# Two-layer gated block on one core: first attention layer and first expert layer rearranged (fills, one-hots, table sums, normalisations, down product)

## The reference, cut to what matters

```python
x = x + tanh(g_xattn[0]) * attn0(layernorm(x), ctx)      # causal, 16 heads of 16, 8 batches of 512 tokens
x = x + tanh(g_ffn[0])   * moe0(layernorm(x))            # 32 experts, top 8, capacity 256, hidden 192, SiLU gate
x = x + tanh(g_xattn[1]) * attn1(layernorm(x), ctx)      # not causal, rows masked
x = x + tanh(g_ffn[1])   * moe1(layernorm(x))            # 8 experts, top 2, capacity 1024, hidden 1024
# moe0: for a token t and each of its 8 experts e: pos = how many earlier tokens chose e
#       buf[e, pos] = x[t]  (dropped at pos >= 256)
#       h = silu(buf @ gate.T) * (buf @ up.T);  out[t] += weight[t, e] * (h @ down.T)[e, pos]
```

## Time and profile before

| | |
|---|---|
| time, median of 3 runs | 2199.86 us (2195.2 to 2203.82) |
| the profiled execution's own time | 2197.13 us |
| its span, first to last instruction | 2195.6 us |
| TensorE busy | 1856.5 us (85%) |
| VectorE busy | 1168.9 us (53%) |
| ScalarE busy | 809.3 us (37%) |
| GpSimd busy | 725.5 us (33%) |
| mean granted clock of TensorE | 0.938 |

### The profile page before, as it was taken

One profiled execution on the slowest core, in us unless ns is written; L12 is line 12 of the kernel. 1 busy time (PEld: TensorE's weight loads), 2 busy tenths in 40 slices (PEclk: granted clock), 3 DMA queues, 4 the chain that ended last, 5 costly groups with the idle time before them and its releaser, 6 DMA issues. The chain is left out here.

```text
span 2195.6 us, 30123 instructions
## 1 busy us (share of the span) xinstructions
PE 1856.5 (85%) x10491; PEld 1039.3 (47%) x10491; DVE 1168.9 (53%) x2966; ACT 809.3 (37%) x1652; POOL 725.5 (33%) x540
## 2 busy tenths in 40 slices
PE   2699999989873888854799999999981999999995
PEld 1345555545442666542234444443331566666664
DVE  3577888887755333333787788878721111212111
ACT  1256555555431222211166666666660111111110
POOL 1212333543344666532112222322113233333322
PEclk9899999999985999977799999999995999999998
DMA  3543334322112888742432244324113323233323
GB/s 92 158 121 103 101 117 141 104 71 89 32 41 90 220 208 221 188 76 89 146 97 85 86 132 128 101 61 132 35 45 93 87 73 77 73 77 77 69 27 96
DMA packets 204245, 222.86 MB, mean 102 GB/s; under 512 B 33438, under 2 KB 195231, under 8 KB 203431
## 3 DMA queue, kind: packets, MB, share of 16 engines
q1 hardware_dynamic: 176458, 177.48, 26.3%
q0 software_dynamic: 27648, 43.60, 10.3%
HBM read 155.06 MB, written 86.93 MB: 110 GB/s over the span
## 5 line engine op out<-in xcount | busy, mean ns | idle before, releaser
L804 DVE TENSOR_REDUCE nmx<-mxb 128x1 f32<-128x512 f32 (+3 forms) x1024 | 585.7, 584 | 212.9 <-PE mxb L657 109.8
L712 ACT ACTIVATE pt<-stb 128x512 f32<-128x512 f32 (+3 forms) x1024 | 499.4, 519 | 365.0 <-PE stb L673 200.4
L657 PE MATMUL mxb<-kst,qst 96*128 96x512 bf16 (+4 forms) x1024 | 355.4, 351 | 62.8 <-DVE nmx L804 52.2
L670 PE MATMUL stb<-qst,kst 99*128 99x512 bf16 (+4 forms) x1024 | 346.4, 345 | 2.1 <-ACT pt L712 1.8
L684 PE MATMUL ob<-pt,va 128*32 128x512 f32 (+3 forms) x2048 | 233.0, 527 | 1.6 <-ACT pt L712 1.1
L1390 PE MATMUL e_h_bank<-e_xT,e_w 128*128 128x512 f32 x512 | 224.8, 598 | 6.1 <-ACT e_xT L1430 5.4
L1404 PE MATMUL e_y_bank<-e_w,e_h 128*128 128x256 f32 x1024 | 226.9, 379 | 0.0
L1071 POOL TENSOR_TENSOR qk<-qk,parts 128x1024 f32<-128x1024 f32 x32 | 68.5, 2139 | 445.9 <-ACT qk L745 224.6
L670 PEld LDWEIGHTS stb<-qst,kst 102*128 102x128 bf16 (+1 forms) x1024 | 99.7, 98 | 235.3 <-ACT pt L712 157.9
L1404 PEld LDWEIGHTS e_y_bank<-e_w,e_h 128*128 128x128 f32 x1024 | 192.9, 190 | 31.8 <-issue 7.2
L1544 POOL DMA_INDIRECT x_after_l<-e_y,e_token x64 | 99.6, 1556 | 282.0 <-DVE e_y L1509 267.3
(11 more groups left out here) (218 smaller groups left out, 2608.0 us busy)
## 6 DMA issues: line engine op xcount, KB each, us to landing
qk_parts<-parts SPq DMA_DIRECT2D x16, 1536.0 KB, 6.0
qst<-qk_parts SPq DMA_DIRECT2D x384, 64.0 KB, 2.3
kst<-qk_parts SPq DMA_DIRECT2D x384, 64.0 KB, 2.3
e_w<-in_L_ffn_w SPq DMA_DIRECT2D x16, 1024.0 KB, 7.4
rows<-rows SPq DMA_DIRECT2D x15, 1060.0 KB, 7.5
crow<-in_ctx SPq DMA_DIRECT2D x16, 512.0 KB, 3.8
x_after_l<-xres SPq DMA_DIRECT2D x16, 512.0 KB, 3.2
e_gu_nat<-in_L_ffn_gate_up_proj SPq DMA_DIRECT2D x64, 128.0 KB, 3.1
```

What stands on the lines that cost most here:

```text
L657: last = pe.matmul(out[:, 0:nk], qst[par][0:rows_used, h, qt * P:(qt + 1) * P], kst[par][0:rows_used, h, 0:nk], start=True, stop=not causal)
L670: last = pe.matmul(out[:, q0:S], kst[par][0:ROWS, h, kt * P:(kt + 1) * P], qst[par][0:ROWS, h, q0:S], start=True, stop=not causal)
L712: act.activation(pt[:, u % 8, q_from(kt):S], stb[(STEPS * b + u) % N_ST][:, q_from(kt):S], ACT.Exp, scale=SCALE).then_inc(s["st_free"], 1)
L804: dve.tensor_reduce(nmx[:, qt, h:h + 1], mxb[(STEPS * n + u) % N_MX][:, 0:k_to(qt)], AX.X, ALU.max, negate=True).then_inc(s["max_free"], 1)
```

## The change

1. Fills: the 15 copies of blank rows leave `experts0`; the list `c.spares` now has 19 entries, and SP issues `c.spares[cur::8]` at the end of iterations 0 to 7 of attention 0.
2. One-hots: GpSimd only subtracts (`differ`: lo in 1024 elements, hi in 512 elements a lane), VectorE compares both with 0 (`one_hot`, two instructions). Tiles 1 and 3 of batch 7 are made on VectorE alone. GpSimd's order becomes `place(done, 1)`, `place(done, 2)`, `low(nn, 1)`, `place(done, 3)`, `norm2(prev)`, in both layers.
3. Table: the four tiles of a batch get their own quarter of one bank, their trips move to steps 18, 20, 22 and 24, and VectorE sums once a batch (`enlist`, step 25) over 256 elements; the tile's number is added and the tiles are summed at the end. `("o", 0, 0)` and `normalise(cur, 0)` move from step 25 to 26.
4. Normalisations: x * rstd + (-mean * rstd), on ScalarE, at steps 16, 17, 18, 20 and 31 to 34, in both layers. VectorE makes -mean, GpSimd the product.
5. Experts of layer 0: `down_(e - 1)` and `result(e - 1)` stand where `down_(e)` and `result(e)` stood.

```diff
-    c.spares = (x1[T:T + CAP0, :], table[T:T + CAP0, 0:D], table[T:T + CAP0, D:W0], x3[T:T + SPARE, :])
+    c.spares = (x1[T:T + CAP0, :], table[T:T + CAP0, 0:D], table[T:T + CAP0, D:W0], x3[T:T + SPARE, :],
+                *(rows1[at_:at_ + SPARE, :] for at_ in range(SPARE, 2 * SLOTS, SPARE)))
...
-    0: ("c", 2, 0, 0, 0), 1: ("c", 2, 1, 0, 1), 7: ("list", -2, 0, 0, 0), 24: ("list", -2, 1, 0, 1),
-    30: ("list", -2, 2, 0, 0), 49: ("list", -2, 3, 0, 0), 3: ("k", 2, 0, 0, 0), ...
+    0: ("c", 2, 0, 0, 0), 1: ("c", 2, 1, 0, 1),
+    18: ("list", -2, 0, 0, 0), 20: ("list", -2, 0, 1, 0), 22: ("list", -2, 0, 2, 0), 24: ("list", -2, 0, 3, 0), ...
...
# SP, end of an iteration
-                if layer == 0 and 0 <= it < len(c.spares):
-                    dst = c.spares[it]
-                    sp.dma_start(dst, c.blank[0:dst.shape[0], 0:dst.shape[1]]).then_inc(c.empty0, 16)
+                if layer == 0 and cur is not None:
+                    for dst in c.spares[cur::B]:
+                        sp.dma_start(dst, c.blank[0:dst.shape[0], 0:dst.shape[1]]).then_inc(c.empty0, 16)
...
# TensorE
-                    pe.wait_ge(s["lo_dve" if dve_made else "lo_pool"], made(b, t))
-                    pe.wait_ge(s["hv_rdy"], 4 * b + t + 1)
+                    pe.wait_ge(s["lo_rdy"], 4 * b + part + 1)
...
# ScalarE
+                    if u in (16, 17, 18, 20) and n3 is not None:
+                        norm1_apply(n3, (16, 17, 18, 20).index(u))
+                    if u in (31, 32, 33, 34) and prev is not None:
+                        norm2_apply(prev, u - 31)
+                last = act.activation(xn[:, i, :], xin[:, i, :], ACT.Identity, bias=shift1[:, i:i + 1], scale=rstd[:, i:i + 1])
...
# VectorE
+            def one_hot(b, t):
                 wait(dve, full["list"], 4 * b + t - 1)
+                if on_dve(b, t):          # batch 7, tiles 1 and 3
+                    dve.tensor_tensor(lo1[...], lanes, lo_f, ALU.is_equal)
+                    dve.tensor_tensor(hv[...], lanes, hi_f, ALU.is_equal)
+                    dve.tensor_scalar(hv[...], hv[...], c.tok1[:, 0:1], None, ALU.mult).then_inc(s["lo_rdy"], 1)
+                else:
+                    dve.wait_ge(s["apart_rdy"], apart(b, t))
+                    dve.tensor_scalar(lo1[t % 2][:, :, :], lo_d[t % 2][:, :, :], 0.0, None, ALU.is_equal)
+                    dve.tensor_scalar(hv[t % 2][:, :, :], hi_d[t % 2][:, :, :], 0.0, c.tok1[:, 0:1],
+                                      ALU.is_equal, ALU.mult).then_inc(s["lo_rdy"], 1)
...
-                        if u in (4, 14, 29, 43):
-                            high(done, (4, 14, 29, 43).index(u))
-                        if u in (8, 24, 30, 49):
-                            enlist(done, (8, 24, 30, 49).index(u))
+                        if u in (4, 14, 19, 23):
+                            one_hot(done, (4, 14, 19, 23).index(u))
+                        if u == 25:
+                            enlist(done)
...
# GpSimd
+            def differ(b, t):
                 pool.wait_ge(s["idx_rdy"], b + 1)
+                wait(pool, s["lo_rdy"], 4 * b + t - 1)
+                pool.tensor_tensor(lo_d[t % 2][:, :, :], lanes_128, lo_f_t, ALU.subtract)
+                pool.tensor_tensor(hi_d[t % 2][:, :, :], lanes_64, hi_f_t, ALU.subtract).then_inc(s["apart_rdy"], 1)
...
                 if done is not None:
                     place(done, 1)
+                    place(done, 2)
                 if nn is not None:
                     low(nn, 1)
                 if done is not None:
-                    place(done, 2)
+                    place(done, 3)
                 if prev is not None:
                     norm2(prev)
-                if done is not None:
-                    place(done, 3)
...
# experts0, TensorE (VectorE's result likewise)
-                down_(e)
+                if e > 0:
+                    down_(e - 1)
+            down_(E0 - 1)
...
-                if e % 2:
-                    for at_ in itertools.islice(fills, 1):
-                        sp.dma_start(rows_next[at_:at_ + SPARE, :], rows_next[0:SPARE, :]).then_inc(s["emptied"], 16)
```

More of the change, by code:

```diff
@@ L291, in attention @@
             lo_f, hi_f = t_("lo_f", [P, NT, 8]), t_("hi_f", [P, NT, 8])
+            lo_d = [t_(f"lo_d{i}", [P, 8, P], BF16) for i in range(2)]
+            hi_d = [t_(f"hi_d{i}", [P, 8, N_HI], BF16) for i in range(2)]
             lo1 = [t_(f"lo1_{i}", [P, 8, P], BF16) for i in range(2)]
-            apart = t_("apart", [P, 8, P], BF16)
             hv = [t_(f"hv{i}", [P, 8, N_HI], BF16) for i in range(2)]
-            listed, part_ = t_("listed", [P, N_HI]), t_("part_", [P, N_HI])
+            listed, part_ = t_("listed", [P, NT, N_HI]), t_("part_", [P, NT, N_HI])
+            found, missing = t_("found", [P, N_HI]), t_("missing", [P, N_HI])
         if layer:
@@ L455, in bank_of, with on_dve, apart @@
             return work[BANK[kind, t]]
-        def made(b, t):
-            if b < B - 1:
-                return 4 * b + t + 1
-            return t // 2 + 1 + (0 if t % 2 else 4 * (B - 1))
+        def on_dve(b, t):
+            return b == B - 1 and t % 2 == 1
+        def apart(b, t):
+            return 4 * b + t + 1 if b < B - 1 else 4 * b + t // 2 + 1
         def rows_of(b):
@@ L635, in trip @@
                 elif kind == "list":
-                    dve_made = b == B - 1 and t % 2
-                    pe.wait_ge(s["lo_dve" if dve_made else "lo_pool"], made(b, t))
-                    pe.wait_ge(s["hv_rdy"], 4 * b + t + 1)
+                    pe.wait_ge(s["lo_rdy"], 4 * b + part + 1)
                     for k in range(8):
-                        done = pe.matmul(out[:, 0:N_HI], lo1[t % 2][:, k, :], hv[t % 2][:, k, :], start=k == 0, stop=k == 7)
+                        done = pe.matmul(out[:, N_HI * part:N_HI * (part + 1)], lo1[part % 2][:, k, :], hv[part % 2][:, k, :],
+                                         start=k == 0, stop=k == 7)
                 else:
@@ L752, in evacuate, with norm1_apply, norm2_apply @@
                     done.then_inc(evac[kind], 1)
+            def norm1_apply(n, i):
+                if i == 0:
+                    act.wait_ge(s["rstd_rdy"], n + 1)
+                    wait(act, full["x"], 2 * n)
+                last = act.activation(xn[:, i, :], xin[:, i, :], ACT.Identity, bias=shift1[:, i:i + 1], scale=rstd[:, i:i + 1])
+                if i == NT - 1:
+                    last.then_inc(s["xn_rdy"], 1)
+            def norm2_apply(b, i):
+                if i == 0:
+                    act.wait_ge(s["rstd2_rdy"], b + 1)
+                    if layer:
+                        wait(act, s[f"scat{b % 2}"], 16 * NSCAT * (b // 2))
+                    else:
+                        wait(act, s["row_out"], 16 * b)
+                last = act.activation(rowb[b % N_ROW][:, i, 0:D], xres[:, i, :], ACT.Identity, bias=shift2[:, i:i + 1],
+                                      scale=rstdb[:, i:i + 1])
+                if i == NT - 1:
+                    last.then_inc(s["row_rdy"], 1)
             def route(b):
@@ L954, in route @@
                 else:
[L955 removed]
+                    wait(dve, s["apart_rdy"], 4 * b)
                     dve.tensor_copy(lo_f[:, :, :], lo_u[:, :, :])
@@ new lines, in enlist @@
+            def enlist(b):
+                got = bank_of("list", 0)[:, 0:NT * N_HI].rearrange("p (t h) -> p t h", t=NT)
+                dve.wait_ge(full["list"], 4 * b + 4)
+                wait(dve, s["lchain"], b)
+                if b:
+                    dve.tensor_scalar(part_[:, :, :], got, 0.0, float(S * b), ALU.is_gt, ALU.mult)
+                dve.tensor_tensor(listed[:, :, :], got, listed[:, :, :], ALU.add).then_inc(evac["list"], 1)
+                dve.wait_ge(evac["list"], b + 1)
+                if b:
+                    dve.tensor_tensor(listed[:, :, :], listed[:, :, :], part_[:, :, :], ALU.add).then_inc(s["lchain"], 1)
+                else:
+                    dve.sem_inc(s["lchain"], 1)
@@ L1016, in _ @@
                         norm2_stats(prev, (23, 24, 26, 27).index(u))
-                    if u == 25 and cur is not None:
+                    if u == 26 and cur is not None:
                         normalise(cur, 0)
@@ L1102, in place @@
                     scatter(b, NSCAT // 4 * quarter, NSCAT // 4 * (quarter + 1))
-                elif b < B - 1 or quarter % 2 == 0:
-                    low_bits(b, quarter)
+                elif not on_dve(b, quarter):
+                    differ(b, quarter)
             for it in ITERATIONS:
@@ L1130, in _, with experts0 @@
                     pool.wait_ge(s[f"scat{par}"], 16 * NSCAT * (B // 2))
-def experts0(c, table, gate_up, down, x, rows_next, token):
+def experts0(c, table, gate_up, down, x, token):
     nc = c.nc
@@ L1166, in _ @@
         def _(sp):
-            fills = iter(range(SPARE, 2 * SLOTS, SPARE))
             for e in range(E0):
@@ L1572, in program @@
```

(2 more changed lines are left out.)

133 lines of the change are left out of this document (56 added, 77 removed), and 2 rows, old and new, of the table TRIPS.

## The result

The changed kernel takes 2211.04 us (median of 6 runs, 2205.22 to 2216.42) against 2198.44 us for the kernel before beside it (2192.42 to 2203.82): a ratio of 1.0059, interval 1.0036 to 1.0083. I had forecast 2190 us. It is slower by 0.6%, a little over the half per cent that I set as the bound (the interval reaches down to 0.4%). So the sign was wrong and the range of 2160 to 2218 held. The profiled execution has a span of 2203.5 us, 7.9 more than before.

The account below looks back on a forecast made before the run. TensorE was taken as the bound, with VectorE's hold-ups showing beyond about 2.2 us in layer 0's attention. Terms -33.5 (experts), +26 (iterations 2 to 7), -2 (tail), 0 (rest) gave -9.5 us: 2190 us, range 2160 to 2218.

Parts of the forecast that it names:

- The forecast mechanism of the one-hots: Layer 0, iterations 2 to 5: VectorE waits for GpSimd's differences, 6.3 us at step 14; TensorE idles 6, then 3 us.
- forecast -33.5: Layer 0 experts: later down product and no fills shorten the stage by 37.3 us, 3.8 lost again at the end.
- forecast +30.2 for iterations 2 to 5: Layer 0 attention: one-hot waits and half clock add 8.4 us to each of iterations 2 to 4, and 5 to iteration 5.
- forecast -7, as -4, -1, -2 and 0: Gains of 4 us in iteration 6, 1 in iteration 7, 2 in layer 0's tail, and nothing in the rest.
- The half clock: Layer 0 attention: TensorE runs at 1.2 GHz after the stalls, counted as 3 us an iteration.
- the experts' chain binds: Rival, chance 0.16: GpSimd's adds land later, the experts' cycle is 7.5 us, 19 us come back, 2209 us.
- the wait for `h` at 26.7 us: Layer 0 experts: TensorE's 0.86 us wait before each down product goes, 26.7 us over 31 cycles.
- the fills' traffic at 10.6: Layer 0 experts: late gathers and the half clock after them, put down to the fills, go: 10.6 us.
- the pair of terms "-4" and "-1": Layer 0 attention: iteration 6 gains 4 us, with GpSimd free at its start; iteration 7 gains 1 us.
- "Rest", put at 0: Layer 1 gains 1 us; ScalarE's wait and an extra product and negation at both layers' starts cost 0.5 each: 0.
- GpSimd isn't late: Rival, chance 0.22: iterations 2 to 5 cost what they did before, since VectorE loses under 2.2 us; 2159 us.
- Half clock decides: Rival, chance 0.20: TensorE stays at 1.2 GHz longer, 4.9 us per stall, +27 us, 2217 us.

Follow-up runs that it names:

- run 3: Kernel before plus only the experts' part: later down product and blank-row copies moved into the first attention layer; 0.9865 of the kernel before.
- run 1: Changed kernel with GpSimd, in layer 0, making the differences of tiles 1 and 2 before norm1 and tile 3's before low(nn, 1); 0.9899 of the kernel before.
- run 9: Kernel before and changed kernel, both unedited, profiled again on one chip; 0.9995 and 1.0042 of the kernel before.
- run 10: Kernel before with the later down product alone, blank-row copies still in the experts' stage; 1.005 of the kernel before.
- run 11: Kernel before with the blank-row copies moved into the first attention layer alone, down product unmoved; 0.9974 of the kernel before.
- runs 4 and 6: Changed kernel with GpSimd's differences earlier in layer 0, plus all normalisations on VectorE (0.9945), or only norm2_apply of iterations 7 and 8 there (0.9875).
- run 2: Changed kernel with both normalisations back on VectorE in both layers, GpSimd's order as changed; 1.0081 of the kernel before.

## Why the prediction was wrong

The forecast mechanism of the one-hots held, and the sum did not. The timed runs alone split it so: -30 us for the experts' part with the fills (run 3; forecast -33.5), +35 for the waits that run 1 removed (forecast +30.2 for iterations 2 to 5), and +7 for all the rest, which is run 1 less run 3 (forecast -7, as -4, -1, -2 and 0). Some 3 us of that +7 are still in iterations 2 to 5. So the step that failed is the rest: the last iterations, and a layer 1 put at nothing. The range held partly by luck, since it was set by the stalls and the clock, and the error came from elsewhere.

In the profiles I had -9.5 us on the span and they have +7.9; on one chip, run 9, the same two kernels have +24.0, in executions 10 us under and 2 over their medians. These are the terms, the first pair before the pair on one chip. (My own sum was 0.8 off: 3 x 8.4 + 5 - 4 - 1 is 25.2, and I wrote 26.)

*One-hots in iterations 2 to 5.* Forecast +30.2 (three times 8.4, and 5); measured 8.1 + 8.3 + 8.9 + 6.2 = 31.5, and 35.7 on one chip. Run 1 shows that it was the two waits and what hangs on them: without them 28 us of it are gone. The hold of each comparison by GpSimd is as I read it from the earlier trace rows. The Trainium skill, "SBUF — State Buffer", section "Who interferes with whom", says the same: VectorE and GpSimd share a port pair that one instruction locks for its whole length. The trace agrees with 2.03 and 1.12 us beside GpSimd, and 0.41 and 0.35 alone in run 1. The half clock cost about the 3 us that I had counted, since a mean clock of 0.96 over 79 us is 6.3 us at 1.2 GHz, but in iteration 3 it followed the first stall only.

*The experts.* Forecast -33.5; measured -43.8 in F and +9.1 until the last add, together -34.7. That this is so near the forecast is luck: on one chip it is -33.8 and +10.3, together -23.5, and timed it is -30. Both terms were mis-sized. The cycle is 6.63 us, not 6.90. The end costs 9.1 and not 3.8 because GpSimd is behind when TensorE finishes: the last add but one starts at 958.28, 5.8 us after its result was there (951.52 + 0.99), and I had it start at once. The rival "the experts' chain binds" is thus true at the end alone; a cycle of 7.5 us isn't there. The split of the gain was wrong in kind. I had the wait for `h` at 26.7 us and the fills' traffic at 10.6, as if each could be had alone. Alone, the later product makes the kernel slower (run 10) and the moved fills give 6 us (run 11); together they give 30 (run 3).

*Iterations 6 and 7: the first step that failed.* It is the pair of terms "-4" and "-1". I wrote them on the ground that GpSimd is free at the start of iteration 6. It is free, and so it makes the differences of tiles 0 and 1 back to back just where VectorE has its chain of short casts: 1.81 us for one of 0.18, and TensorE waits 3.55 us for `m` in iteration 7, 2.5 more than before. In iteration 6 the same chain has a cast of 1.59 us, and TensorE waits 2.32 us behind `maxima`. No run moved these differences, so the price of this hold is read from rows and not tested. In iteration 7 `norm2_apply` on ScalarE comes on top, 4.6 to 5.1 us (57.2 against 52.6 and 52.1 in runs 4 and 6), which is tested. Measured +0.6 and +7.0, together 12.6 worse than forecast; on one chip 15.5 worse.

*"Rest", put at 0: the second.* I had taken layer 1 for a place where TensorE is busy anyway and costed ScalarE's normalisations as work between exponentials. That holds where TensorE has `maxima` to do too (0.3 us an iteration measured). In the last iterations it hasn't, and a step with both takes ScalarE 0.97 us. The first pair of profiles gives +17.5 us for layer 1's periods, the pair on one chip +10.1, and runs 1 and 3, on the chip without pauses, +3.0 (443.1 against 440.1). Of this, run 2 bears out about 3 us (52.4 for period 6 against 55.8 in run 1). GpSimd's order in layer 1, which the change alters too, had no term in my sum at all; run 9 shows that on two chips the fifth period is longer with it, 2.5 us in the pair. The rest of the same-chip difference is not settled. G, cleared of the later last add, fell by 6.9 us in the first pair and by about 1 in the other, so I count no gain there.

*Start and tail.* -3.0 to the first exponential, less than the 5.0 by which the changed kernel's own profiles differ; in the last period and the way to the experts -4.5 in the first pair and -5.3 on one chip, where I had -2. Some 2 us of these need not be the change's: the last period is 46.8 and 46.5 in the kernel before and 44.7 in runs 10 and 11, which have the old table too.

The rival "GpSimd isn't late" is refuted by the 6.29 us. "Half clock decides" gave the sign, but not by its mechanism: the clock cost about what was counted. The result fell between my forecast and that rival, through terms that I had set near zero or below.

## What to carry to other kernels

Before an in-order queue of one engine is made to wait for another, look where the other one idles: here 8.54 us of idle time stood ahead of the work that was waited for, and moving two calls into it and a third forward gave 35 us. A pipeline's first and last iterations need a costing of their own, since the engine that covers a load in the full ones is missing there. Of two edits that each remove one of two near-equal limits, each alone can be worth little or make it slower, here +0.5% and -0.3%, where both give -1.4%. And rows of single executions can differ, for one kernel, by as much as the term that is looked for: price a term by timed runs where they can be had.

## What the runs showed of the hardware

GpSimd's back-to-back instructions hold even VectorE's shortest ones: a cast of 32 elements a lane, 0.18 us alone, took 1.81, and a subtraction of 32 elements a lane with two operands, 0.19 in run 1 with GpSimd idle, took 0.98. In the profiles of two chips ScalarE paused 3.0 us between two exponentials at the same place of iteration 7 of layer 1, in either kernel, around the end of a run of indirect transfers issued by GpSimd and with no cause in the trace; on a third chip it never did. Layer 1's periods of the kernel before differ by 7.3 us between its two profiles (437.4 and 444.8), so it is worth having both kernels on one chip. A ScalarE normalisation of 128x256 shows 0.59 us, hardly less than the 0.69 of a 128x512 bias addition, but in a row with exponentials the next one starts 0.49 us behind it.
